# Attention blocks in chunk-major order with all keys on chip, and token sums through VectorE's bank ring

## The chip, the core and the metric
The kernel runs on one core of a Trainium2 chip. The metric is device time in microseconds of one execution. Three executions of the kernel before took 906.76, 907.65 and 915.72 us (median 907.65). The profiled execution took 914.75 us; its span, from the first to the last recorded instruction, is 913.0 us.

## The reference, cut to what matters
One transformer layer over 2048 tokens of width 256, all in float32. The input is normalised; on the normalised rows `xn` stand a causal attention with 16 heads of width 16 (rotary positions, softmax, output projection) and a mixture of experts (32 experts of inner width 128; six per token out of four of eight groups) with a shared expert:

```python
x = L0_attn_x                                  # (1, 2048, 256)
xn = _layernorm(x, axis=-1)
x = x + _L0_attn_ref(xn, Wqkv, Wout) + _L0_ffn_ref(xn, gate_w, w11, w33, w22, sw1, sw2, sw3)
# attention: softmax(causal(q k^T / 4)) v, heads merged, times Wout^T
# experts: sigmoid gates, six experts per token, silu(x w11) * (x w33) * c, times w22, summed
```

## The kernel before, in words
**Stages.** First the projections, tile by tile (16 tiles of 128 tokens), from 12 to 140 us of the profile. Queries and keys are rotated and each is split into three bf16 terms; these go to DRAM (`term_rows`) and come back transposed, as 96 rows of terms per head (`load_terms`, L420). Values stay in `v_all`. Then attention, in two lots with the experts between them: `attend(early)`, the experts, `attend(late)`.

**Attention.** Heads are worked in 4 groups of 4 (`g`), queries in 4 chunks of 512 (`c`), keys in blocks of 128 (`kb`). A key block of (g, c) has four score matmuls `st` (L1173, a mask by L1176 on the diagonal), each followed by an exponential on ScalarE (L710), and a value product `pv` (L1190, eight matmuls; weights are 32 columns of `V4`, the values of the group in hand). There are 160 blocks, here group by group: chunk (g, c) has 4(c+1) blocks. Before the blocks of a chunk its row maxima must be known. They come from `strips(g, c)`: score matmuls with queries as rows (`mx`, L1149, mask L1152) whose maxima VectorE takes (L955), 8(c+1) strips a chunk, 320 in all. `mc` combines them, `mt` turns them into three extra rows of the queries (copy L977). After the last block of a chunk ScalarE copies the sums (`oe`), TensorE turns them (`ot`), VectorE divides (L994, L996). At a change of group ScalarE copies the next group's values to `V4` (`take_v`, `v4`), and TensorE's first product of the group waits for it.

**The order.** All engines walk one list, written by `whole_order` (L96): between every two `st` steps stand those strips, token steps and output steps that are due by goals (`score_goals`, `token_goals`, `end_goals`), and two steps of a chain of routing and slot computation (`route`, `counts`, `ranks`, `slots`, `owner`; VectorE and TensorE in turn) until that is used up. The strips of chunk (0, 0) and eight chain steps stand ahead of the first block. Blocks are counted from 0 in this list. The experts stand before block 64.

**Banks.** Eight PSUM banks: two pairs as VectorE's ring (`d_ring`), banks 4 and 5 for `st` and the exponentials, bank 6 for value products, bank 7 for counts, ranks and, through blocks 8 to 50, the token sums. `banks_in_turn` (L186) gives bank 7 to the exponentials after the step `tokens`.

**Tokens.** GpSimd makes one-hot tiles from the slots (L568, L569, twelve instructions a token tile, four tiles of buffer). TensorE sums products of them over the 16 token tiles in bank 7 (`tok`, L1218, six matmuls a tile), VectorE casts the sum to `tok_i` (L1001). GpSimd's gathers of rows for the experts (L587) start from it. After the experts GpSimd adds the expert rows to `res` (L602). `oM` (L989) waits for them; these output steps begin at block 146.

**Buffers.** `turned` holds one group's queries and two groups' keys. SyncE loads the next group's queries chunk by chunk when `used` (L432) says the old ones are done, and the keys a group ahead.

## Time and profile before

| | us |
|---|---|
| median of three executions | 907.65 |
| profiled execution, its span | 914.75, 913.0 |
| projections until the first exponential | 0 to 144.2 |
| blocks 0 to 63 | 144.2 to 394.6 |
| experts | 394.6 to 617.7 |
| blocks 64 to 159 and the end | 617.7 to 913.0 |
| busy TensorE, VectorE, GpSimd, ScalarE | 836.4, 605.6, 505.1, 497.1 |

Busy time is recorded time of instructions; TensorE's matmuls are pipelined, so its rows overlap and include some waiting. The number after `x` is a count. A time in square brackets or after the bar is the idle time of the engine before the instruction, with what ended it. `PEclk` is TensorE's granted clock as a share of 2.4 GHz.

### The profile page before, as it was taken

The numbers are of one execution on the slowest core, as the hardware profiler recorded it, in microseconds if no ns is written. First come the engines' busy times: TensorE is split into PE (matmuls) and PEld (weight loads), VectorE is DVE, ScalarE is ACT, GpSimd is POOL, SyncE is SP. The second block draws the span as 40 slices with busy tenths as digits, with TensorE's granted clock in tenths as the row PEclk, the third lists the DMA queues.
The fourth block names the chain that finished last, engine by engine and source line by source line (L and its number), as shares of the span: only waits on it lengthen the run. The fifth ranks groups of instructions, "written<-read, shape, count | busy, mean of one in ns | idle before, by whom it ended". The sixth has DMA issues, their size and how long they took to land.

```text
span 913.0 us, 17558 instructions
## 1 busy us (share of the span) xinstructions
PE 836.4 (92%) x5281; PEld 455.5 (50%) x5282; DVE 605.6 (66%) x1179; ACT 497.1 (54%) x1214; POOL 505.1 (55%) x651
## 2 busy tenths in 40 slices
PE   5799977698989998989999999998999999999997
PEld 2466644233343433368888887773343343433444
DVE  2677776888876686755555555555788777888322
ACT  3556523155556655635444544456676756667672
POOL 3566640499989302046666666626878888810000
PEclk9999987799999999999999999999999999999999
DMA  7025554610000212037777777774585555510011
GB/s 222 1 78 175 172 175 138 165 32 19 1 19 1 67 44 64 1 102 229 234 234 227 225 244 229 140 140 71 74 170 87 72 90 72 88 18 1 13 35 47
DMA packets 81986, 96.15 MB, mean 105 GB/s; under 512 B 13030, under 2 KB 73446, under 8 KB 81894
## 3 DMA queue, kind: packets, MB, share of 16 engines
q0 software_dynamic: 19968, 31.47, 19.1%
q1 hardware_dynamic: 45033, 46.80, 17.3%
q10 hardware_dynamic: 16896, 16.78, 5.4%
q8 instruction: 45, 0.74, 0.3%
q14 instruction: 44, 0.36, 0.1%
HBM read 61.11 MB, written 33.82 MB: 104 GB/s over the span
## 4 chain that ended last, share of the span: by engine, by line
PE 68%; issue 14%; DVE 10%; SPq 2%; ACT 2%; DVEq 1%; DMA 1%; POOLq 1%; POOL 1%; ACTq 0%
PE bank L1190 13%; PE bank L1173 13%; PE vector_banks L1149 11%; PE vector_banks L1268 7%; DVE mpart L955 7%; PE vector_banks L1041 5%; PE vector_banks L1062 4%; PE bank L1281 3%; PE bank L1062 3%; PE bank L1041 2%; PE vector_banks L1210 2%; PE bank L1078 2%; PE bank L1176 1%; PE vector_banks L1152 1%; ACT probs L710 1%
## 5 line engine op out<-in xcount | busy, mean ns | idle before, releaser
L955 DVE TENSOR_REDUCE mpart<-vector_banks 128x2 f32<-128x1024 f32 (+3 forms) x320 | 330.7, 1062 | 100.8 <-PE vector_banks L1149 58.2
L710 ACT ACTIVATE probs<-bank 128x512 f32<-128x512 f32 (+3 forms) x428 | 213.5, 537 | 136.7 <-PE bank L1176 64.7
L1173 PE MATMUL bank<-turned 99*128 99x512 bf16 (+3 forms) x640 | 207.2, 355 | 17.4 <-ACT probs L710 5.3
L587 POOL DMA_INDIRECT turned<-normed_rows,tok_i x128 | 125.6, 981 | 138.6 <-PE vector_banks L1041 85.1
L1149 PE MATMUL vector_banks<-turned 96*128 96x512 bf16 (+3 forms) x640 | 185.3, 360 | 12.8 <-DVE mpart L955 12.2
L602 POOL DMA_INDIRECT res<-expert_rows,slot_i x96 | 148.9, 1551 | 43.3 <-issue 28.6
L1173 PEld LDWEIGHTS bank<-turned 99*128 99x128 bf16 x640 | 58.9, 97 | 186.2 <-ACT probs L710 86.6
L710 ACT ACTIVATE at_first<-bank 128x512 f32<-128x512 f32 (+3 forms) x212 | 106.2, 532 | 74.4 <-PE bank L1176 35.6
L1268 PE MATMUL vector_banks<-xn_all,probs 128*128 x512 | 136.3, 389 | 3.0 <-issue 1.3
L1190 PE MATMUL bank<-probs,V 128*32 128x512 f32 (+3 forms) x856 | 102.2, 549 | 0.0
L1268 PEld LDWEIGHTS vector_banks<-xn_all,probs 128*128 128x128 f32 x512 | 87.8, 191 | 16.0 <-issue 7.7
L1019 DVE SCALAR_TENSOR_TENSOR probs<-probs,vector_banks 128x128 f32<-128x128 f32 x128 | 36.9, 288 | 83.9 <-ACT probs L724 46.6
L615 ACT ACTIVATE probs<-bank 128x128 f32<-128x128 f32 (+1 forms) x256 | 83.5, 328 | 16.2 <-PE bank L1281 1.9
L724 ACT ACTIVATE probs<-vector_banks 128x128 f32<-128x128 f32 x128 | 35.6, 278 | 102.4 <-PE vector_banks L1268 85.4
L1149 PEld LDWEIGHTS vector_banks<-turned 96*128 96x128 bf16 x640 | 59.3, 101 | 59.0 <-DVE mpart L955 24.8
L568 POOL TENSOR_SCALAR turned<-turned 128x128 f16<-128x128 f16 x96 | 58.0, 604 | 45.4 <-DVE turned L936 42.2
L569 POOL TENSOR_SCALAR turned<-turned 128x128 f16<-128x128 f16 x96 | 76.9, 801 | 0.0
L1281 PE MATMUL bank<-xn_all,probs 128*128 x256 | 76.7, 382 | 0.0
L1013 DVE COPY probs<-vector_banks 128x256 f32<-128x256 f32 x128 | 53.5, 418 | 1.9 <-PE vector_banks L1041 1.3
L1176 PE MATMUL bank<-mask_k,identb 128*128 128x128 bf16 x256 | 54.6, 223 | 0.0
L1152 PE MATMUL vector_banks<-mask_q,identb 128*128 128x128 bf16 x256 | 53.5, 228 | 0.0
L1023 DVE SCALAR_TENSOR_TENSOR probs<-probs,slot_w,vector_banks 128x128 f32<-128x128 f32 x128 | 44.6, 348 | 10.8
(152 smaller groups left out, 967.8 us busy)
## 6 DMA issues: line engine op xcount, KB each, us to landing
expert_rows<-probs ACTq DMA_DIRECT2D x32, 512.0 KB
term_rows<-at_first SPq DMA_DIRECT2D x96, 128.0 KB
turned<-term_rows SPq DMA_DIRECT2D x32, 384.0 KB, 5.0
xn_all<-wexp SPq DMA_DIRECT2D x32, 384.0 KB
normed_rows<-xn_all SPq DMA_DIRECT2D x4, 512.0 KB, 5.5
turned<-normed_rows,tok_i POOLq DMA_INDIRECT x128
out<-res SPq DMA_DIRECT2D x16, 128.0 KB, 1.7
res<-x SPq DMA_DIRECT2D x1, 1536.0 KB, 9.2
```

The costliest lines, as they stand in the source:

```text
L569: last = gp.tensor_scalar(hi_hot[t % HOT][:, j, :], count_from_0[:, :], hi[:, t, j:j + 1], token[:, t:t + 1], ALU.is_equal, ALU.mult)
L587: gp.indirect_dma_start(xg[:, n % XR, :], None, xn_dram, bass.IndirectOffsetOnAxis(ap=tok_i[:, n:n + 1], axis=0)).then_inc(rows_in[n % XR] ...
L602: gp.indirect_dma_start(res[:, t, :], None, yg_dram, bass.IndirectOffsetOnAxis(ap=slot_i[:, t, j:j + 1], axis=0), compute_op=ALU.add).then ...
L615: return A(dst, src, ACT.Copy)
L710: A(PT[v // 2 % 6][:, v % 2, 0:width], bank[A_BANK[step][0]][:, 0:width], ACT.Exp).then_inc(s["scalar_bank_read"], 1)
L955: V.tensor_reduce(mpart[:, t % TPC, 2 * j:2 * j + 2, p], ring[:, :, 0:w], AX.X, ALU.max).then_inc(s["vector_bank_read"], 1)
L1041: return nc.tensor.transpose(dst, src, eye)
L1149: last = mm(ring[:, h, 0:w], q_turned(slice(0, KQ), 2 * j + h, t * P, P), k_turned(par, slice(0, KQ), 2 * j + h, p * CH, w), start=True, s ...
L1173: last = mm(ring[:, 0:CH - off], k_turned(parity(g), slice(0, KM), h, kb * P, P), q_turned(slice(0, KM), h, c * CH + off, CH - off), start ...
L1190: last = mm(pv_bank[VW * h:VW * (h + 1), off:CH], V4[:, kb, h, :], PT[(2 * v + h // 2) % 6][:, h % 2, 0:CH - off], start=kb == 0, stop=kb ...
L1268: last = mm(bank[2 + n % 2][:, 0:2 * INTER], xgT[n % 2][:, c, :], wt_flat[:, bass.ds(at + c * D, D)], start=c == 0, stop=c == DC - 1)
L1281: mm(bank[6 + n % 2][:, 0:D], ehT[n % 2][:, :], wt_flat[:, bass.ds(at + 2 * D, D)], start=True, stop=True).then_inc(s["y_done"], 1)
```

## The change
Key blocks go chunk by chunk: for each chunk c all four groups, then the next chunk. The keys of all groups and chunks have room of their own (`keys`); queries lie in four slots (`queries`, slot = (4c + g) mod 4), and a slot is loaded again when the blocks of the chunk four back are issued. The values are written once, by the projections, in rows of 17 words a head (16 values and a one), so `V4`, its copies and `v4` go; a value product takes 32 columns from a head's start. Token sums go through VectorE's ring: eight steps, each two token tiles in a ring bank, added to `tok_sum` by VectorE. Bank 7 goes to the exponentials after the last slot step, which stands at block 2. Goals are new: token steps from block 8 to 64; strips by chunk; experts before block 72. SyncE's loads are in the order of the new use. Buffers of early stages lie in other places. `V` of VectorE's program is called `VE`. The core of the diff:

```diff
-TOKENS_FROM, TOKENS_TO = 8, 50
-EXPERTS_AT = (1, NCH - 1)
+TOKENS_FROM, TOKENS_TO = 8, 64
+EXPERTS_AT = (2, NCH - 2)
...
-    key_blocks = [(g, c, kb) for g in range(NG) for c in range(NCH) for kb in range(TPC * (c + 1))]
+    key_blocks = [(g, c, kb) for c in range(NCH) for g in range(NG) for kb in range(TPC * (c + 1))]
     scores, score_goals = [], [(0, 0)]
...
+    for c in range(NCH):
+        for g in range(NG):
+            if c or g:
+                scores += strips(g, c)
+                if c == 0 or g in (0, NG - 1):
+                    score_goals.append((4 * key_blocks.index((g, c, 0)) - 6, len(scores)))
+    tokens = [("tok", u) for u in range(NT // 2)]
...
-            if pending[1] == NCH - 1:
-                order.append(("v4", pending[0] + 1))
...
-        if step[0] == "tokens":
+        if step == ("slots", SLOT_PIECES - 1):
             free.insert(0, 7)
...
-                copy(v_all[:, bass.ds(t, 1), :].rearrange("p a n -> p (a n)"), bank[3 + b][:, 0:D])
+                copy(V[:, t, 0:H * V1].rearrange("p (h v) -> p h v", v=V1)[:, :, 0:DH],
+                     bank[3 + b][:, 0:D].rearrange("p (h d) -> p h d", d=DH))
...
-                            last = mm(pv_bank[VW * h:VW * (h + 1), off:CH], V4[:, kb, h, :],
+                            last = mm(pv_bank[VW * h:VW * (h + 1), off:CH], V[:, kb, (HG * g + h) * V1:(HG * g + h) * V1 + VW],
...
+                    elif step[0] == "tok":
+                        u = step[1]
+                        dve.wait_ge(s["vector_bank_full"], n + 1)
+                        dve.drain()
+                        if u == 0:
+                            VE.tensor_copy(tok_sum[:, :], ring[:, 0, 0:SLOT_TILES]).then_inc(s["vector_bank_read"], 1)
+                        else:
+                            VE.tensor_tensor(tok_sum[:, :], tok_sum[:, :], ring[:, 0, 0:SLOT_TILES], ALU.add).then_inc(s["vector_bank_read"], 1)
+                        if u == NT // 2 - 1:
+                            dve.drain()
+                            VE.tensor_copy(tok_i[:, :], tok_sum[:, :]).then_inc(s["tok_ready"], 1)
...
+                if quarter == 0:
+                    sp.wait_ge(s["terms_stored"], 16 * STORES)
+                    for g in range(NG):
+                        load_keys(g, 0)
+                        load_queries(g, 0)
...
+            sp.wait_ge(s["terms_stored"], 16 * STORES * 4)
+            sp.wait_ge(ones_in[0], 16)
+            for c in (1, 2):
+                for g in range(NG):
+                    load_keys(g, c)
+                set_ones(c)
+                if c == 1:
+                    store_weights(3)
...
+            def next_queries(some):
+                for i in some:
+                    used(*chunks[i - Q_SLOTS])
+                    load_queries(*chunks[i])
+
             sp.wait_ge(s["plan_ready"], 1)
+            sp.wait_ge(s["weights_stored"], 16 * 4)
+            next_queries([Q_SLOTS])
+            for g in range(NG):
+                load_keys(g, NCH - 1)
+            set_ones(NCH - 1)
...
-                        if t == 0:
-                            pe.wait_ge(s["owner_row_ready"], 1)
-                        pe.wait_ge(s["hot_made"], t + 1)
-                        for j in range(TOPK):
-                            last = mm(gu_bank[:, 0:SLOT_TILES], lo_hot[t % HOT][:, j, :], hi_hot[t % HOT][:, j, :],
-                                      start=t == 0 and j == 0, stop=t == NT - 1 and j == TOPK - 1)
-                        last.then_inc(s["hot_used"], 1)
+                        u = step[1]
+                        for t in (2 * u, 2 * u + 1):
+                            pe.wait_ge(s["hot_made"], t + 1)
+                            for j in range(TOPK):
+                                last = mm(ring[:, 0, 0:SLOT_TILES], lo_hot[t % HOT][:, j, :], hi_hot[t % HOT][:, j, :],
+                                          start=t == 2 * u and j == 0, stop=t == 2 * u + 1 and j == TOPK - 1)
+                        last.then_inc(full, 1)
```

## Rows read from the trace of the kernel before

**Rows 1.** The page: busy time by engine, clock in 40 slices, one DMA group.
```profile
PE 836.4 (92%) x5281; PEld 455.5 (50%) x5282; DVE 605.6 (66%) x1179; ACT 497.1 (54%) x1214; POOL 505.1 (55%) x651
...
PEclk9999987799999999999999999999999999999999
...
turned<-term_rows SPq DMA_DIRECT2D x32, 384.0 KB, 5.0
```

**Rows 2.** Busy time by stretch: from:to, length, engines (count), clock, DMA share, GB/s.
```profile
144.20:179.70 35.50, 24.54 (x153) 11.44 (x153) 26.72 (x62) 7.00 (x16) 8.32 (x13) 0.76 0.62 176
...
258.00:339.90 81.90, 76.52 (x579) 31.13 (x578) 59.70 (x75) 50.82 (x101) 44.52 (x67) 1.00 0.14 33
...
737.40:810.10 72.70, 69.30 (x522) 28.40 (x521) 58.32 (x73) 49.15 (x102) 53.99 (x35) 1.00 0.52 77
810.10:900.00 89.90, 87.89 (x603) 37.20 (x601) 44.41 (x62) 61.83 (x131) 0.00 (x0) 1.00 0.06 19
```

**Rows 3.** The exponentials (L710) alone by stretch: ScalarE's busy time and count.
```profile
144.20:195.80 51.60, 16.12 (x33) 0.80 0.49 143
...
258.00:339.90 81.90, 48.50 (x97) 1.00 0.14 33
...
737.40:810.10 72.70, 47.09 (x98) 1.00 0.52 77
```

**Rows 4.** The strips' maxima (L955) alone by stretch: VectorE's busy time and count.
```profile
144.20:195.80 51.60, 30.66 (x31) 0.80 0.49 143
195.80:227.70 31.90, 23.33 (x23) 1.00 0.05 14
...
258.00:339.90 81.90, 50.85 (x50) 1.00 0.14 33
...
737.40:810.10 72.70, 50.14 (x49) 1.00 0.52 77
```

**Rows 5.** The timeline of the opening: start, duration, instruction, idle before it.
```profile
152.15 3.40 PE L1232 MATMUL bank<-at_first,onesb 128*128 128x480 bf16 x15 [1.78 <-DVE at_first L893]
...
160.35 3.00 SPq L423 DMA_DIRECT2D turned<-term_rows  x6
...
171.38 0.62 POOL L568 TENSOR_SCALAR turned<-turned 128x128 f16<-128x128 f16 x1 [42.15 <-DVE turned L936]
```

**Rows 6.** Groups of instructions, 144.2 to 195.8: count, busy us, mean ns, idle before.
```profile
L1149 PE MATMUL vector_banks<-turned 96*128 96x512 bf16 (+3 forms) x64 | 20.8, 403 | 5.9 <-DVE mpart L955 5.9
...
L955 DVE TENSOR_REDUCE mpart<-vector_banks 128x2 f32<-128x1024 f32 x20 | 24.0, 1222 | 9.7 <-PE vector_banks L1149 9.3
L955 DVE TENSOR_REDUCE mpart<-vector_banks 128x2 f32<-128x768 f32 x3 | 2.9, 950 | 0.1
L955 DVE TENSOR_REDUCE mpart<-vector_banks 128x2 f32<-128x512 f32 x4 | 2.8, 688 | 0.7 <-PE vector_banks L1152 0.6
L955 DVE TENSOR_REDUCE mpart<-vector_banks 128x2 f32<-128x256 f32 x4 | 1.7, 420 | 0.5 <-PE vector_banks L1152 0.4
```

**Rows 7.** The timeline at the first change of group.
```profile
317.08 1.05 ACT L615 ACTIVATE V<-v_all 128x1024 f32<-128x1024 f32 x1
...
318.57 0.28 PE L1173 MATMUL bank<-turned 99*128 99x256 bf16 x1 [1.05 <-ACT at_first L710]
```

**Rows 8.** Groups of GpSimd, 170 to 340, and TensorE's token matmuls, 258.0 to 339.9.
```profile
L569 POOL TENSOR_SCALAR turned<-turned 128x128 f16<-128x128 f16 x96 | 76.9, 801 | 0.0
L568 POOL TENSOR_SCALAR turned<-turned 128x128 f16<-128x128 f16 x96 | 58.0, 604 | 45.4 <-DVE turned L936 42.2 <-PE bank L1218 3.2
...
L1218 PE MATMUL bank<-turned 128*128 128x128 f16 x54 | 4.5, 218 | 0.0
```

**Rows 9.** Value weight loads of a block (timeline), and VectorE's division group, 640 to 800.
```profile
200.74 0.16 PEld L1190 LDWEIGHTS bank<-probs,V 128*32 128x32 f32 x8 [0.42 <-ACT probs L710]
...
L996 DVE TENSOR_TENSOR v_all<-vector_banks,rden 128x256 f32<-128x256 f32 x5 | 2.1, 425 | 0.4
```

**Rows 10.** VectorE's timeline after the token list is made.
```profile
347.85 0.42 DVE L955 TENSOR_REDUCE mpart<-vector_banks 128x2 f32<-128x256 f32 x1 [2.83 <-issue]
```

More of the change, by code:

```diff
@@ L160, in whole_order @@
                 values(block)
-            order.append(later.pop()[1])
+            order += [step for _, step in later]
+            later.clear()
             pending = []
@@ L257, in carve @@
             return take
-        turned = sb("turned", [P, 2 * HG * T])
+        KW = NG * HG * CH // 2
+        keys = sb("keys", [P, NCH * KW])
+        queries = sb("queries", [P, Q_SLOTS * HG * CH // 2])
         probs = sb("probs", [P, 4 * 2 * CH])
-        QW = HG * T // 2
-        EARLY_WORDS = 15360
-        first_words = sb("at_first", [P, EARLY_WORDS])
-        at_first = carve(first_words, EARLY_WORDS)
-        before = carve(turned[:, 2 * QW:3 * QW], QW)
-        routing = at_first
-        counting = carve(turned[:, 3 * QW:], QW)
-        ffn = carve(turned[:, 3 * QW:], QW)
+        o_words = sb("o_words", [P, NT * D])
+        more_words = sb("more_words", [P, 3840])
+        spare = sb("spare", [P, 3456])
+        at_first = carve(o_words, NT * D)
+        staging = [carve(keys[:, c * KW:(c + 1) * KW], KW) for c in (2, 1)]
+        routing = carve(keys[:, 3 * KW:], KW)
+        before = carve(more_words, 3840)
+        counting = carve(spare, 3456)
+        ffn = carve(spare, 3456)
         before_probs = carve(probs, 4 * 2 * CH)
@@ L276, in layer @@
         qk = [at_first([P, 2 * D]) for b in range(2)]
-        split = [at_first([P, SPLIT, 2 * D], BF16) for b in range(2)]
+        split = [staging[b]([P, SPLIT, 2 * D], BF16) for b in range(2)]
         left = at_first([P, 2 * D])
-        staged = [at_first([P, SPLIT, COLS, CH], BF16) for b in range(2)]
-        v_all = sb("v_all", [P, NT, D])
-        o_all = v_all
+        staged = [staging[b]([P, SPLIT, COLS, CH], BF16) for b in range(2)]
+        V = sb("values", [P, NT, VROW])
+        o_all = o_words[:, :].rearrange("p (t d) -> p t d", d=D)
         ident = sb("ident", [P, P])
@@ L447, in _ @@
                                          staged[quarter % 2][:, n, 2 * kind + half, :]).then_inc(s["terms_stored"], 16)
-                sp.wait_ge(s["terms_stored"], 16 * STORES * (quarter + 1))
-                for kind in range(2):
-                    load_terms(kind, 0, quarter)
+                if quarter == 0:
[3 more added lines that the diff above has]
+                        load_queries(g, 0)
             def load(e, b, first=False):
@@ L475, in _ @@
                 load(b, b, True)
-            for c in range(NCH):
-                used(0, c)
-                load_terms(0, 1, c)
-            for c in range(NCH):
-                load_terms(1, 2, c)
-            for c in range(NCH - 1):
-                used(1, c)
-                load_terms(0, 2, c)
+            ready = chunks.index(EXPERTS_AT) + Q_SLOTS
+            next_queries(range(Q_SLOTS + 1, ready))
             with sp.Fori(1, E // NB) as i:
@@ L486, in _ @@
                     load(NB * i + b, b)
-            used(1, NCH - 1)
-            load_terms(0, 2, NCH - 1)
-            for c in range(NCH):
-                load_terms(1, 3, c)
-            for c in range(NCH):
-                used(2, c)
-                load_terms(0, 3, c)
+            next_queries(range(ready, len(chunks)))
             for t in range(NT):
@@ L791, in shared_add @@
                 row = res[:, bass.ds(t, 1), :].rearrange("p a n -> p (a n)")
-                V.tensor_tensor(row, row, bank[6][:, 0:D], ALU.add).then_inc(s["shared_added"], 1)
+                VE.tensor_tensor(row, row, bank[6][:, 0:D], ALU.add).then_inc(s["shared_added"], 1)
             def statistics(tiles, part):
@@ L832, in route @@
                 for t in each:
[L833 removed]
+                    VE.max(out=top[:, t, :], in_=gx[:, t, :])
                 dve.drain()
```

242 lines of the change are left out of this document (113 added, 129 removed).

## The prediction, made before the changed kernel was run
> **What bounds the kernel now.** I read the page first. TensorE is busy 92% of the span, more than any other engine, and its clock is granted in full except at slices 9 to 12 [rows 1]. So the span is TensorE's own instruction stream plus the places where that stream stands still, and the question is where it does. I cut the attention into stretches by counting exponentials, four for each key block (a count of 97 or 98 is 24 blocks and one or two caught at the edges). Blocks 0 to 7 take 51.6 us, blocks 8 to 15 take 31.9, blocks 24 to 47 take 81.9 (27.3 for each eight) [rows 3, 4]. The same 24-block pattern (the last chunk of one group, then the first two of the next) returns after the experts, in blocks 104 to 127, and takes 72.7 us there. There the exponentials own three banks; before block 50 they own two. In both stretches VectorE reduces 49 or 50 strips for about 50.5 us [rows 4], and TensorE's busy share is 0.93 and 0.95 [rows 2]. So TensorE is paced by bank returns as much as by its work.
>
> The opening is another thing. Of its first 35.5 us TensorE has work for 24.5, at a mean clock of 0.76 [rows 2]. VectorE carries 31 strips in blocks 0 to 7, 20 of them of the widest form at 1222 ns, besides the chain of routing and slot steps; TensorE stands 5.9 us before strips for want of a returned bank [rows 4, 6]. The chain crosses between the two engines, the 15 rank matmuls take 3.40 us, and GpSimd gets its slots only at 171.38 [rows 5].
>
> **The change, term by term.** Total strips, exponentials and value products are the same; only their order changes, so each term is a stall removed or added. Terms are given with a value and both ends.
>
> Opening, blocks 0 to 7: **-14 us (-5 to -16)**. Counted from the new order, 19 strips stand beside these blocks instead of 31: eight of group 1, eight of group 2, three of group 3, all of chunk 0. By the forms' means (1222, 950, 688 and 420 ns, [rows 6]) they cost VectorE 14.7 us where it now spends 30.7 [rows 4]: 16 us less. The low end is the 5.9 us that TensorE visibly stands before strips, less one for what stays. I take nearly the high end, since VectorE works 26.7 of the first 35.5 us and the chain runs through it [rows 2]; 2 us stay with the waits for ranks and counts.
>
> Giving back the strips: **+8 us (+4 to +13)**. By block 16 the old order has done 54 strips beside blocks, the new one 43. Eleven wide strips must be done later. The price of a strip in a full stretch: blocks 8 to 15 have 23 strips and take 31.9 us, a third of the stretch of blocks 24 to 47 has 16.7 and takes 27.3, so 4.6 us for 6.3 strips, 0.73 us each, 8 in all. Ends: 0.4 us if only TensorE's columns count, 1.22 if VectorE's whole duration does.
>
> Third bank for blocks 8 to 49: **-10 us (0 to -16)**. The pair of stretches differs by 9.2 us in 24 blocks. The early one also holds 54 token matmuls (nine tiles; I take 0.056 us from start to start of these 128-column ones, so 3.0 us) [rows 8] and a strip more (0.5). These 5.7 us are 0.24 us for a block, 10 for 42 blocks. The high end is all 9.2 us (0.38 a block), the low end is nothing, if VectorE's ring is what binds.
>
> Group copies of values: **-3 us (0 to -3.2)**. Three times, at a change of group, ScalarE copies the group's values for 1.05 us in line with exponentials, and TensorE stands 1.05 us before its next score matmul [rows 7]. They go. The strided copy into the new layout in the projections takes the old copy's place on ScalarE; I cost it at nothing.
>
> Token sums in VectorE's ring: **+3 us (0 to +5)**. There are eight sums. The nearest row is a VectorE pass over 256 columns at 425 ns [rows 9]; with its drain say 0.5, 4 us of VectorE, most of which TensorE feels, since each also takes a ring place ahead of a strip. Behind the waiting sum on VectorE stand strips and maxima, and for these TensorE waits in turn. The 96 token matmuls stay.
>
> Uneven strips: **+2 us (0 to +5)**. The new goals put four strips to a block in blocks 11 to 14, three in 39 to 46, 2.7 in 83 to 94: 24 above the even two. The old order has the same 24 surplus, in blocks 0 to 23. Only the spacing is new, hence little.
>
> First token sum: **+2 us (0 to +5)**. It now needs two tiles of one-hots before block 8 goes on. GpSimd needs 12 instructions of 604 and 801 ns a tile, 8.4 us, 16.9 for two, after the slots are ready [rows 8]. Blocks 3 to 7 are small ones that take some 15 us by this sum. TensorE would stand the rest, with strips and exponentials queued behind.
>
> At nothing: SyncE's loads. It issues six loads of keys in 3.00 us [rows 5]; the new order has eight after the first quarter, hidden by the wait for the next quarter's terms, and later eight keys ahead of chunk 1's strips, which begin at block 10, some 20 us on. Chunk 3's keys, four weight loads and the queries follow, each for a use tens of us away; without that cover a load would cost its 5.0 us from issue to landing [rows 1]. The experts start at block 72 instead of 64: that moves the combining of rows on GpSimd some us later, but GpSimd is idle from 810.1 on [rows 2], so outputs that begin at block 146 still find them done. The stall when the gathers start after the token list (VectorE stands 2.83 us before 347.85) merely moves [rows 10].
>
> The sum is -14 + 8 - 10 - 3 + 3 + 2 + 2 = **-12 us**. The profiled execution took 914.75 us (span 913.0), 7.1 above the median of 907.65; a like execution would take 902.75, and the median becomes **895.7 us**.
>
> **A rule on the clock.** TensorE's granted clock is 0.76 over the first 35.5 us of the opening, a mean of its levels of 1.2 and 2.4 GHz, in a stretch where it is busy 69% [rows 2]; elsewhere it is 1.00. The Trainium skill (TensorE: Matmul & The Clock Gate, What's actually happening) says that the throttled state is the default and activity releases it. By that rule, taking strips out of the opening makes TensorE idler there, and the remaining work would run at 1.2 GHz for longer. An estimate by it: some 18 us of TensorE work left beside blocks 0 to 3 at 0.76 would be 27 at 0.50, and with half of the 9 us showing, 4 of the first term are lost, a sum of -8. I keep -12 because VectorE is what TensorE waits for there.
>
> **Rivals.** (a) *VectorE sets the pace, the third bank gives nothing.* For it: VectorE is busy 59.7 of 81.9 us in the two-bank stretch [rows 2], and idle TensorE time before strips names it. Against: the fast stretch has the same strips. Then the third term is 0: -2, **905.7 us**. (b) *More than forecast*: the whole 9.2 us is the banks' (-16) and strips come back at 0.4 us (+4): -22, **886 us**. For it: TensorE's busy records cover waits. Against: the token matmuls are real work. (c) *Slower, by the value rows.* The value products' weights come from rows 68 bytes apart by head instead of from an aligned block. Eight loads now take 0.16 us a block [rows 9]. If these doubled on TensorE's path, 160 blocks add 26 us: -12 + 26 = +14, **921.7 us**. Slower by over 1% needs 21 us, 0.13 a block. Against: they overlap the products. The Trainium skill (SBUF — State Buffer, Door 1: The DMA port swizzle) puts a penalty on each new 16-byte line; an estimate by it is nine lines for eight, 3 us in all. No row here shows that. (d) *Not what it says.* The third bank needs the slot chain's end, which is at block 2 in the order; if a wait held it back the time is that of (a).
>
> **Chances.** Forecast 0.50 (own range 888 to 903), (a) with (d) 0.27, (b) 0.12, (c) 0.11. About 1% (9 us) is what a measurement here can tell from no change. Faster by more: below 898.6, about 0.7 of the forecast, all of (b), a little of (a): 0.50. Slower by more: (c) and the bad ends of the terms: 0.12. Same: 0.38. The range with 8 in 10 runs from (b)'s 886 to **909**, leaving out (c) and the tail below (b).
>
> **What would show it.** Blocks 0 to 7 at 38 us (wrong above 47); 24 blocks with two strips a block before the experts at 75 us instead of 82, with token sums in them; no copies of values and no stand after them; GpSimd's first one-hot near 162 (some 9 of the opening's 14 us lie ahead of it). Wrong: eight value weight loads above 0.25 us; TensorE waiting for keys or queries; one wait of over 5 us at the first token sum; late stretches slower than 24.5 us for eight blocks.

## The result and the profile after

The changed kernel takes **911.42 us** (median of 20 executions, 908.07 to 917.19) against 908.03 for the kernel before (20 executions). The ratio is 1.0036 (95%: 1.0020 to 1.0051). The forecast was 895.7. So nothing was gained, and by the ratio some 3 us were lost, less than counts as a change here. The profiled execution took 912.08 us, its span is 910.2.

The two spans, 913.0 and 910.2, seem to tell of a gain. They don't: the profiled execution of before, 914.75 us, lies 6.7 above its kernel's median. A second one took 907.21 us (span 905.3). The largest difference between the two is in blocks 48 to 55. By stretch (from:to, length, then busy time and count of TensorE, its weight loads, VectorE, ScalarE and GpSimd, clock, DMA share, GB/s), first the execution that the prediction read:

```profile
339.90:367.70 27.80, 23.91 (x158) 8.74 (x156) 17.41 (x19) 14.98 (x35) 8.95 (x13) 0.94 0.21 58
```

and the same eight blocks in the second execution:

```profile
338.50:360.10 21.60, 21.60 (x161) 8.42 (x159) 17.12 (x19) 14.89 (x33) 8.96 (x13) 1.00 0.27 75
```

These 6.2 us belong to one execution and not to the kernel.

**Where the time went.** The start of the first exponential of a block, by counting exponentials as in [rows 3], gives this ledger (us; in brackets the second profiled execution of each kernel, where it differs by more than 1):

| blocks | before | after | difference |
|---|---|---|---|
| 0 to 7 | 51.6 (51.2) | 35.8 (39.5) | -15.8 (-11.7) |
| 8 to 15 | 31.9 | 34.6 | +2.7 |
| 16 to 31 | 58.2 (60.0) | 50.9 (52.6) | -7.3 |
| 32 to 47 | 54.0 | 62.5 (60.4) | **+8.5** (+6.5) |
| 80 to 95 | 45.6 | 56.9 | **+11.3** |
| 96 to 127 | 96.5 | 94.4 | -2.1 |

The rest is -3.3 (+1.6) for blocks 48 to 79 with the experts and +3.5 (+2.1) from block 128 to the end. At block 32 the changed kernel is 20 us ahead (17 in the second pair). It loses most of them in two stretches of 16 blocks.

Equal block numbers are not equal work everywhere. A diagonal block has narrower matmuls and exponentials than a full one. Of blocks 0 to 31, 8 are full in the new order and 20 in the old (0 and 4 of blocks 0 to 7); the new order has four more full ones in each of blocks 48 to 79, 96 to 127 and 128 to 159. So a part of the 20 us is work put off, and no run here prices it alone. In blocks 32 to 47 and 80 to 95 both orders have 8 full and 8 diagonal blocks, so those two rows compare like with like. The page after, to be laid beside [rows 1]:

```profile
PE 832.5 (91%) x5281; PEld 460.8 (51%) x5282; DVE 604.1 (66%) x1187; ACT 494.1 (54%) x1210; POOL 502.6 (55%) x651
...
PEclk9999988999998999989999999998999999999998
...
keys<-term_rows SPq DMA_DIRECT2D x16, 384.0 KB, 8.8
```

All engines work about as long as before. What is new is in the clock's row. The 7, 7 at slices 7 and 8 of before are gone (an 8, 8 stands at slices 6 and 7), but there is an 8 at slices 13, 18, 28 and 40, where there was none: at 273 to 296 us, in the dense blocks 32 to 47, on both sides of the experts, and at the end. By stretch, the kernel after:

```profile
143.90:179.70 35.80, 27.60 (x260) 15.99 (x259) 25.25 (x70) 13.66 (x34) 17.77 (x27) 0.90 0.79 206
179.70:214.30 34.60, 29.44 (x272) 15.22 (x269) 29.10 (x43) 14.56 (x35) 34.13 (x51) 1.00 0.36 96
214.30:265.20 50.90, 47.16 (x385) 21.31 (x384) 37.42 (x51) 30.82 (x67) 39.84 (x60) 1.00 0.06 17
...
327.70:376.90 49.20, 46.63 (x345) 18.96 (x343) 37.44 (x46) 33.32 (x67) 8.95 (x13) 1.00 0.15 41
...
652.50:709.40 56.90, 52.05 (x363) 20.41 (x361) 48.28 (x55) 30.66 (x66) 47.75 (x31) 0.97 0.55 80
```

In the second profiled execution of the changed kernel, blocks 0 to 7 and 32 to 47 read:

```profile
142.00:181.50 39.50, 30.64 (x261) 17.66 (x259) 25.38 (x70) 13.74 (x34) 18.46 (x28) 0.80 0.82 205
268.30:328.70 60.40, 51.84 (x401) 22.37 (x399) 47.66 (x59) 32.31 (x68) 37.39 (x55) 1.00 0.05 14
```

So the opening's clock of 0.90 (first row of the stretches) belongs to one execution, and blocks 32 to 47 are long (60.4 us) at full clock too. Blocks 80 to 95 before:

```profile
668.00:713.60 45.60, 44.31 (x337) 18.46 (x335) 38.73 (x45) 32.07 (x69) 36.25 (x24) 1.00 0.70 128
```

The strips' maxima alone, after (VectorE's busy time and count), to be read against [rows 4]:

```profile
143.90:179.70 35.80, 14.34 (x19) 0.90 0.79 206
...
214.30:265.20 50.90, 31.03 (x33) 1.00 0.06 17
265.20:327.70 62.50, 41.12 (x41) 0.95 0.04 14
652.50:709.40 56.90, 43.31 (x41) 0.97 0.55 80
```

and the two stretches of before that the last two replace:

```profile
285.90:339.90 54.00, 36.02 (x34) 1.00 0.19 45
668.00:713.60 45.60, 34.83 (x33) 1.00 0.70 128
```

The stretches that lost time are those that got more strips: 41 in 16 blocks instead of 34 and 33. VectorE is busy 48.3 of 56.9 us there. Blocks 96 to 127, with two strips a block in both kernels, take 2.1 us less than before.

**What stands in such a stretch.** The longest stand of the exponentials in the trace after is at the end of chunk (2, 1): diagonal blocks, whose score matmuls are the smallest, with the widest strips between them, and the turning of the next chunk's maxima right behind. The timelines of TensorE, VectorE and ScalarE (start, duration, instruction, idle before it):

```profile
288.05 0.23 PE L1175 MATMUL vector_banks<-keys,queries 96*128 96x128 bf16 x1 [1.61 <-DVE mpart L975]
...
289.18 1.87 PE L1068 MATMUL vector_banks<-identb,mcat 128*3 128x128 bf16 x16 [0.72 <-DVE mpart L975]
...
286.78 2.67 DVE L975 TENSOR_REDUCE mpart<-vector_banks 128x2 f32<-128x1024 f32 x3
...
291.41 0.28 ACT L734 ACTIVATE probs<-bank 128x128 f32<-128x128 f32 x1 [4.66 <-PE bank L1199]
```

TensorE's instructions stand in the trace in the order of the list. A strip that waits for a ring bank holds back the next score matmul behind it, and ScalarE, with three banks free, stands 4.66 us. A third exponential bank can't help here: what holds the score matmul up is ahead of it in the queue. The bank comes late because VectorE has just combined the next chunk's maxima (L984 to L993, 285.39 to 286.86) and then has three of the widest maxima, 2.67 us, to take. In this execution TensorE, having stood 1.61 and 0.72 us, goes on at a lower clock:

```profile
288.00:291.00 3.00, 2.23 (x21) 1.84 (x22) 1.45 (x2) 0.00 (x0) 3.00 (x6) 0.59 0.00 0
291.00:296.00 5.00, 5.00 (x29) 1.74 (x32) 3.20 (x3) 1.31 (x4) 3.24 (x5) 0.56 0.11 30
```

Clock 0.56 is close to 1.2 of 2.4 GHz: by an estimate from this row (5.00 times 0.56), what TensorE does in these last 5 us would take some 2.8 at full clock. The second execution has the same stands, 1.60 and 0.72 us, and no slow stretch behind them; its turn of the maxima takes 1.05 us instead of 1.87, and ScalarE stands 3.73 us:

```profile
292.24 1.05 PE L1068 MATMUL vector_banks<-identb,mcat 128*3 128x128 bf16 x16 [0.72 <-DVE mpart L975]
```

The stand belongs to the order, the dip to the execution. The dip is worth about 2 of the 8.5 us; 6.5 remain without it.

### The profile page after: what moved, and what is told of

The parts are those of the page before. It is cut to its first block, busy times and chain, and to the rows that moved or that the text cites. A ratio compares the mean times of both kernels' runs of the same rounds, so it can differ in the third digit from the quotient of the medians.

```text
span 910.2 us, 17585 instructions
## 1 busy us (share of the span) xinstructions
PE 832.5 (91%) x5281; PEld 460.8 (51%) x5282; DVE 604.1 (66%) x1187; ACT 494.1 (54%) x1210; POOL 502.6 (55%) x651
## 4 chain that ended last, share of the span: by engine, by line
PE 75%; DVE 14%; issue 4%; DMA 3%; DVEq 2%; POOLq 1%; ACT 1%; POOL 0%; SPq 0%; ACTq 0%
PE bank L1212 14%; PE bank L1196 12%; PE vector_banks L1289 12%; DVE mpart L975 10%; PE vector_banks L1175 10%; PE vector_banks L1068 7%; PE bank L1302 6%; PE vector_banks L1089 4%; PE bank L1089 3%; PE bank L1068 2%; DMA xn_all<-wexp 2%; PE vector_banks L1232 2%; DVEq L983 2%; PE bank L1105 2%; PE vector_banks L1178 1%
## 5 line engine op out<-in xcount | busy, mean ns | idle before, releaser
L975 DVE TENSOR_REDUCE mpart<-vector_banks 128x2 f32<-128x1024 f32 (+3 forms) x320 | 326.6, 1061 | 93.3 <-PE vector_banks L1175 72.5
L734 ACT ACTIVATE probs<-bank 128x512 f32<-128x512 f32 (+3 forms) x428 | 215.8, 541 | 125.5 <-PE bank L1199 73.9
L1196 PE MATMUL bank<-queries,keys 99*128 99x512 bf16 (+3 forms) x640 | 205.5, 354 | 8.4 <-DVE owner_row L960 3.5
L614 POOL DMA_INDIRECT spare<-normed_rows,tok_i x128 | 125.3, 979 | 130.3 <-PE vector_banks L1068 84.1
L1175 PE MATMUL vector_banks<-keys,queries 96*128 96x512 bf16 (+3 forms) x640 | 182.7, 355 | 13.5 <-DVE mpart L975 10.4
L734 ACT ACTIVATE more_words<-bank 128x512 f32<-128x512 f32 (+3 forms) x212 | 106.4, 526 | 86.0 <-PE bank L1199 60.1
L1196 PEld LDWEIGHTS bank<-queries,keys 99*128 99x128 bf16 x640 | 61.2, 97 | 172.0 <-ACT probs L734 75.7
L1212 PE MATMUL bank<-probs,values 128*32 128x512 f32 (+3 forms) x856 | 104.7, 561 | 0.0
L595 POOL TENSOR_SCALAR spare<-spare 128x128 f16<-128x128 f16 x96 | 57.3, 597 | 65.4 <-DVE spare L956 33.0
L1175 PEld LDWEIGHTS vector_banks<-keys,queries 96*128 96x128 bf16 x640 | 60.1, 100 | 62.5 <-DVE mpart L975 22.7
L596 POOL TENSOR_SCALAR spare<-spare 128x128 f16<-128x128 f16 x96 | 76.2, 794 | 0.0
```

The lines of the kernel that those rows point to most:

```text
L596: last = gp.tensor_scalar(hi_hot[t % HOT][:, j, :], count_from_0[:, :], hi[:, t, j:j + 1], token[:, t:t + 1], ALU.is_equal, ALU.mult)
L614: gp.indirect_dma_start(xg[:, n % XR, :], None, xn_dram, bass.IndirectOffsetOnAxis(ap=tok_i[:, n:n + 1], axis=0)).then_inc(rows_in[n % XR] ...
L734: A(PT[v // 2 % 6][:, v % 2, 0:width], bank[A_BANK[step][0]][:, 0:width], ACT.Exp).then_inc(s["scalar_bank_read"], 1)
L975: VE.tensor_reduce(mpart[:, t % TPC, 2 * j:2 * j + 2, p], ring[:, :, 0:w], AX.X, ALU.max).then_inc(s["vector_bank_read"], 1)
L1175: last = mm(ring[:, h, 0:w], q_turned(slice(0, KQ), g, 2 * j + h, t * P, P), k_turned(slice(0, KQ), g, 2 * j + h, p * CH, w), start=True, ...
L1196: last = mm(ring[:, 0:CH - off], k_turned(slice(0, KM), g, h, kb * P, P), q_turned(slice(0, KM), g, h, c * CH + off, CH - off), start=True ...
```

## The experiments

The theories. **Spacing**: the strips bunched in blocks 32 to 47 and 80 to 95 eat the gain, since VectorE takes over 1 us for each and blocks with fewer strips give nothing back. **Bank**: the third bank is worth less than forecast. **Lateness**: strips end only a few score steps ahead of their chunk, and the turn of maxima waits. Ratios are to the kernel before in the same round on the same chip, with the 95% interval; 0.001 is 0.9 us.

**The changed kernel again**, as the measure for the first four.

> The changed kernel itself, unchanged, so that the others have a time and a trace of it on the same chip. Both theories: 1.003 to 1.005 of the kernel before, within 3 us of it.

Measured: 913.11 us, 1.0046 (1.0024 to 1.0068).

**Even strips.** Most goals are left out, so that the planner spreads the strips evenly between those that stay: 17 or 18 for each eight blocks from block 16 to 95, nowhere more than 10 for four, where the changed kernel has up to 12. It also has four strips more in blocks 0 to 7 (23) and three fewer in blocks 8 to 15 (21).

```diff
-                if c == 0 or g in (0, NG - 1):
+                if (g, c) in ((1, 0), (0, 1), (0, 2), (0, 3), (NG - 1, NCH - 1)):
```

> The changed kernel with the strips spread evenly: goals only at chunks (1,0), (0,1), (0,2), (0,3) and (3,3), so that from block 16 no eight blocks hold more than 18 strips (the changed kernel has 22 in blocks 40 to 47, and 20 and 20 in 80 to 95). Theory A (above some 2.3 wide strips a block VectorE sets the pace, and each surplus strip costs its whole 1.22 us or more, which sparse stretches do not give back): 8 to 16 us faster than the changed kernel, about 897; blocks 32 to 47 take 54 us instead of 62.5, blocks 80 to 95 take 48 to 50 instead of 56.9. Theory B (the loss is TensorE's work moved out of the opening and costs the same wherever it stands): within 3 us of the changed kernel, about 911.

Measured: 902.57 us, 0.9926 (0.9902 to 0.9949), so 0.0120 or **10.9 us** below the changed kernel on the same chip, and faster than the kernel before. It was run twice more on another chip:

> The evenly spread kernel once more, unchanged, as the base of the other three on this chip, and for a trace nearer its median (the first was of its slowest execution). Expected: 0.990 to 0.996 of the kernel before, blocks 32 to 47 at 54 us, 80 to 95 at 50 us.

> The evenly spread kernel, unchanged, on the chip of the three below: their base. 0.988 to 0.994 of the kernel before.

Measured: 898.30 us, 0.9875 (0.9844 to 0.9905), and 901.55 us, 0.9921 (0.9892 to 0.9950). Each of its three profiled executions was the slowest of its series (910.66, 903.21 and 905.57 us), so its traces rather understate the gain. By stretch, blocks 0 to 7, 8 to 15, 16 to 31, 32 to 47, 48 to 63 of the second:

```profile
145.60:184.40 38.80, 29.65 (x275) 17.23 (x273) 28.14 (x74) 13.72 (x33) 20.78 (x31) 0.91 0.81 204
184.40:216.60 32.20, 27.39 (x256) 14.02 (x254) 27.06 (x40) 14.30 (x35) 31.75 (x48) 1.00 0.30 85
...
216.60:269.10 52.50, 48.41 (x396) 22.01 (x397) 41.07 (x55) 30.32 (x66) 38.15 (x57) 1.00 0.06 16
269.10:323.70 54.60, 50.65 (x387) 21.64 (x386) 44.06 (x55) 30.78 (x66) 40.24 (x59) 0.97 0.06 16
323.70:373.40 49.70, 47.76 (x350) 18.88 (x349) 39.63 (x48) 32.72 (x66) 8.95 (x13) 1.00 0.16 40
```

and its maxima in blocks 32 to 47 and 80 to 95:

```profile
269.10:323.70 54.60, 37.84 (x37) 0.97 0.06 16
650.30:700.50 50.20, 37.29 (x35) 1.00 0.56 80
```

The gain is where it should be: 54.6 us instead of 62.5 (60.4 in the second execution) with 4 strips fewer, 50.2 instead of 56.9 with 6 fewer. What was moved into blocks 16 to 31 (37 instead of 33 strips, 2.3 a block) costs 52.5 - 50.9 = 1.6 us there, 0.4 a strip. The even kernel also turns some maxima earlier, 7 to 14 score steps ahead of their chunk where the changed one has 3; the last experiment takes that away.

**Bunching doubled.** The strips of chunks (2, 3) and (3, 3) are done in the first half of the blocks that precede them. The strips are the same in all, 61 or 62 in blocks 112 to 143.

```diff
-                if c == 0 or g in (0, NG - 1):
+                if (g, c) in ((2, NCH - 1), (3, NCH - 1)):
+                    score_goals.append((4 * key_blocks.index((g - 1, c, 0)) + 26, len(scores)))
+                    score_goals.append((4 * key_blocks.index((g, c, 0)) - 6, len(scores)))
+                elif c == 0 or g in (0, NG - 1) or (g, c) == (1, NCH - 1):
```

> The changed kernel with the strips of chunks (2,3) and (3,3) done in the first half of the blocks before them: blocks 109 to 119 and 125 to 134 get up to four strips a block, blocks 121 to 125 and 136 to 143 none; the work is the same. Theory A: some 19 strips above the pace, each 1.2 us of which the empty blocks give back 0.4 to 0.5: 12 to 20 us slower than the changed kernel. Theory B: within 3 us of it.

Measured: 936.54 us, 1.0306 (1.0279 to 1.0332), **23.6 us** above the changed kernel. Its blocks 112 to 119, 120 to 127, 128 to 135 and 136 to 143:

```profile
756.90:796.30 39.40, 32.02 (x184) 10.33 (x184) 32.32 (x36) 19.03 (x34) 33.00 (x22) 0.96 0.52 72
796.30:817.50 21.20, 18.82 (x126) 5.67 (x125) 4.57 (x5) 14.51 (x33) 9.37 (x7) 1.00 0.33 44
817.50:855.10 37.60, 30.51 (x187) 10.15 (x191) 32.03 (x36) 19.10 (x34) 0.00 (x0) 1.00 0.00 1
855.10:872.90 17.80, 16.22 (x112) 4.50 (x112) 0.00 (x0) 13.97 (x34) 0.00 (x0) 1.00 0.00 1
```

the maxima in the first:

```profile
756.90:796.30 39.40, 29.16 (x28) 0.96 0.52 72
```

(28 again in blocks 128 to 135, none behind them) and the same 32 blocks in the changed kernel:

```profile
756.90:849.70 92.80, 89.50 (x607) 33.00 (x606) 71.56 (x78) 65.34 (x131) 42.65 (x28) 1.00 0.29 42
```

116.0 us against 92.8, and this accounts for the whole loss. By the same eight blocks, the changed kernel takes 22.5, 24.7, 22.5 and 23.4 us, with 17, 17, 17 and 14 maxima taken in them. Eleven more cost 16.9 and 15.1 us, **1.4 to 1.5 each**: VectorE's 1.22 for the widest form [rows 6], and something more. Twelve and 14 fewer give back 3.5 and 5.6 us, 0.3 to 0.4 each, near the 0.4 at which the prediction put TensorE's columns. The price has a knee: up to about 2.3 strips a block (the even kernel above) a strip costs 0.4 us or less, at 3.5 a block more than its time on VectorE. Blocks 32 to 47 and 80 to 95 of the changed kernel, with up to three, stand on the dear side.

**The third bank withheld** until the last token step, in the changed kernel (a) and in the even one (b):

```diff
-        if step == ("slots", SLOT_PIECES - 1):
+        if step == ("tok", NT // 2 - 1):
```

> The changed kernel with bank 7 given to the exponentials only after the last token sum (block 57), not after the slots (block 2): the third bank taken away alone. If the third bank is worth what the prediction says (0.24 us a block): 10 to 13 us slower than the changed kernel, blocks 16 to 31 at 56 us instead of 50.9. If VectorE's ring sets the pace before the experts: within 2 us of the changed kernel.

> The even kernel with the third bank withheld until the last token sum (block 57). If the third bank's worth was hidden in the changed kernel by VectorE's dense stretches, it shows here: 5 us or more slower than the even kernel. If a third bank is worth little before the experts however the strips lie: 2 to 3 us slower, as in the changed kernel.

Measured: (a) 915.66 us, 1.0073 (1.0046 to 1.0101), beside the changed kernel's 1.0046: 2.5 us, with some 3 us either way by the two intervals. (b) 908.22 us, 1.0000 (0.9972 to 1.0028), beside the even kernel's 0.9875 in the same series: 11.3 us; beside its 0.9926 and 0.9921 in the two other series it would be 7. By stretch, (a), blocks 16 to 31, 32 to 47, 48 to 63:

```profile
215.50:268.10 52.60, 48.73 (x385) 20.40 (x383) 37.77 (x51) 31.78 (x66) 39.86 (x59) 1.00 0.06 16
268.10:330.90 62.80, 54.39 (x401) 22.46 (x399) 47.91 (x59) 32.87 (x67) 38.92 (x58) 0.97 0.05 13
330.90:383.80 52.90, 49.87 (x345) 19.04 (x343) 37.59 (x45) 34.22 (x66) 8.95 (x13) 0.97 0.14 39
```

(b), the same blocks:

```profile
219.00:274.60 55.60, 50.88 (x397) 21.63 (x397) 41.59 (x56) 31.79 (x66) 38.56 (x57) 1.00 0.05 15
274.60:331.40 56.80, 52.44 (x387) 21.74 (x386) 44.11 (x55) 32.02 (x66) 39.67 (x59) 0.97 0.05 15
331.40:383.20 51.80, 49.52 (x351) 18.64 (x349) 40.04 (x48) 33.63 (x67) 8.94 (x13) 1.00 0.15 39
```

By stretch the bank gives 1.7, 0.3 and 3.7 us in (a), in all 5.7, and 3.1, 2.2 and 2.1 in (b), in all 7.4. Against the second trace of the changed kernel (a) reads 0.1, 2.4 and 3.7. Without the bank TensorE stands 2.1 us before score matmuls in (a) and 4.2 in (b), between 180 us and the experts; with it 0.0 in both kernels. So the bank is worth less than forecast in the changed kernel, and more in the even one by the ratios. That dense strips are the reason fits this, but the stretches don't single them out, and single traces set the two only 2 us apart: it is likely and not shown.

**The ring and the bank in the old order**: the kernel before, group by group, with the token sums in VectorE's ring and bank 7 given away after the last slot step.

```diff
-    tokens = [("tok", t) for t in range(NT)] + [("tokens",)]
+    tokens = [("tok", u) for u in range(NT // 2)]
...
-        if step[0] == "tokens":
+        if step == ("slots", SLOT_PIECES - 1):
```

> The kernel before, group by group as it is, with one part of the change alone: token sums in eight steps through VectorE's ring, and bank 7 to the exponentials after the slots (block 3). By the prediction's terms (third bank -10 us, sums +3): 7 us faster than the kernel before, 0.992. If the third bank is worth only the 2.6 us that its removal from the changed kernel cost, against the same sums: within 2 us of the kernel before. Blocks 24 to 47 (81.9 us before) show it: 76 by the first, 80 to 82 by the second.

> The kernel before, profiled once more, since its first profiled execution lay 7 us above its median. Expected: a span of 905 to 908 us; the stretch of blocks 48 to 63, which held the stand at 347 us, 4 to 6 us shorter than the 54.7 us of the first trace; the opening within 2 us of 51.6.

Measured: 904.96 us, 0.9966 (0.9941 to 0.9990), **-3.1 us**, where the terms of the prediction give -7 (-10 and +3). The gain stands where there are two strips a block (24 to 47), none where there are nearly three (8 to 15):

```profile
197.50:229.70 32.20, 27.95 (x213) 11.68 (x212) 26.91 (x33) 15.70 (x34) 31.72 (x48) 1.00 0.05 14
259.90:337.80 77.90, 73.35 (x574) 30.95 (x573) 60.59 (x79) 48.68 (x101) 56.72 (x84) 1.00 0.17 44
```

against 31.9 and 81.9 us [rows 2 to 4] (83.4 in the second execution). In the 24 blocks from which the prediction read 5.7 us for the bank, bank and sums together give 4.0 (5.5), so that reading was sound; it did not hold for the other blocks.

**The chunk-major order alone, evenly spaced**: bank 7 keeps the token sums and goes to the exponentials after the last of them, at block 60.

```diff
-    tokens = [("tok", u) for u in range(NT // 2)]
+    tokens = [("tok", t) for t in range(NT)] + [("tokens",)]
...
-        if step == ("slots", SLOT_PIECES - 1):
+        if step[0] == "tokens":
```

> The evenly spread kernel with the token sums back in bank 7 and so only two banks for the exponentials until block 64: both halves of that part of the change undone together. By the prediction's terms: 8 to 10 us slower than the even kernel with ring sums, about 912. If bank and sums pay for each other: within 3 us of it, about 903.

Measured: 903.87 us, 0.9970 (0.9948 to 0.9993): the order alone gives -2.7 us. Ring and bank together bring 4 to 9 us more, by the even kernel's 0.9926, 0.9921 and 0.9875 in other series. It also stands 0.0030 below (b), which differs from it in that the sums go through the ring, and in that the bank comes at block 57, not 60: 2.7 us for the eight sums, though the intervals overlap and the two ran in different series.

**Goals counted in TensorE's time** instead of steps (a diagonal step weighs 0.6).

```diff
+    for g, c, kb in key_blocks:
+        pace += [pace[-1] + (i + 1) * (6 if kb >= TPC * c else 10) for i in range(4)]
...
-            upto = len(steps) if everything else max(done, due(goals, at))
+            upto = len(steps) if everything else max(done, due(goals, pace[at] if steps is scores else at))
```

> The evenly spread kernel with goals in TensorE's time instead of steps: a step of a diagonal block counts 0.6 of a step of a full one, so that the four diagonal blocks at a chunk's end, where VectorE also has the maxima and the turned rows, hold 5 to 7 strips and the full ones 9 to 11 for every four. If VectorE's load in short stretches sets the pace: 3 to 7 us faster than the even kernel, about 898. If eight-block evenness is all that counts: within 2 us of it, about 903.

Measured: 905.38 us, 0.9978 (0.9955 to 1.0001). That is worse than all three results of the plain even kernel. So leaving diagonal blocks fewer strips gains nothing.

**Strips back into the opening.** Even kernel with six strips moved from blocks 8 to 15 into blocks 0 to 7 (29 and 16 instead of 23 and 22).

```diff
+    score_goals.insert(2, (22, 24))
```

> The even kernel with the 24 strips of chunk 0 due by block 5 instead of block 10: blocks 0 to 7 hold 29 strips, not 23, and blocks 8 to 15 hold 15, not 21; all else alike. If strips in the opening cost VectorE's time there (the prediction's first term) and blocks 8 to 15 are held by VectorE too, the two cancel: blocks 0 to 7 about 5 us longer, 8 to 15 about 5 us shorter, in all within 2 us of the even kernel. If the opening's gain is real gain and the later blocks don't give back: 3 to 5 us slower than the even kernel.

Measured: 903.17 us, 0.9943 (0.9924 to 0.9963), 6.2 us above the even kernel of that series, 2 above it by the two others. Its two stretches:

```profile
146.40:197.70 51.30, 38.19 (x312) 22.31 (x311) 35.88 (x86) 13.97 (x34) 32.38 (x48) 0.81 0.73 185
197.70:222.40 24.70, 22.93 (x223) 11.96 (x220) 19.50 (x28) 13.68 (x35) 19.48 (x30) 1.00 0.17 50
```

Beside 38.8 and 32.2 us: +12.5 and -7.5, so 2.1 us a strip in the opening (clock 0.81 against 0.91) and 1.25 in blocks that have nearly three each. But the even kernel's two other traces have 42.5 and 42.6 us for blocks 0 to 7, at clock 0.81, and 33 to 34 us for 8 to 15; beside these it is about +9 and -9, 1.5 us a strip on both sides. So a strip costs more than its time on VectorE in both places. The ratios make the emptier opening a gain of 2 to 6 us; the traces leave it between 0 and 5, according to the clock that the opening got.

**Goals two blocks earlier**, the dense stretches kept (as many strips in them as in the changed kernel), and **both cures together**.

```diff
-                    score_goals.append((4 * key_blocks.index((g, c, 0)) - 6, len(scores)))
+                    ahead = 6 if c == 0 or (g, c) == (0, 1) else 14
+                    score_goals.append((4 * key_blocks.index((g, c, 0)) - ahead, len(scores)))
```

> The changed kernel with its dense stretches kept, but every goal from chunk (1,1) on eight steps earlier, so that maxima are turned 6 to 11 score steps ahead of their first use, not 3. Rival to theory A: the even kernel gained because maxima are ready earlier. Then this is 5 us or more faster than the changed kernel, below 908. By theory A only density counts: within 3 us of the changed kernel (about 1.004 of the kernel before); blocks 32 to 47 and 80 to 95 stay at 59 to 62 and 56 us.

> The changed kernel with dense stretches kept and goals eight steps earlier, unchanged from its first run (0.9893), as a repeat on this chip: 0.987 to 0.993. If it were 1.00 or more, its first result would not stand for the kernel.

> Both at once: even spread, and from chunk (0,2) on goals eight steps earlier, so maxima stand ready 11 to 22 score steps ahead. If density and lateness are two costs that add: 3 to 8 us faster than the even kernel, about 0.983. If both cures remove the same stand of TensorE at a chunk's end: within 2 us of the better of the two.

Measured: early goals 897.77 us, 0.9893 (0.9864 to 0.9922), and 898.45 us, 0.9905 (0.9874 to 0.9937): as good as even strips. The spacing theory alone forecast about 1.004 for them, so it is not the whole. Both together 903.00 us, 0.9937 (0.9903 to 0.9971): not better. The dense stretches with early goals, blocks 32 to 47 and 80 to 95:

```profile
265.20:324.10 58.90, 51.79 (x399) 22.02 (x398) 47.52 (x59) 32.02 (x66) 40.25 (x60) 1.00 0.05 14
645.90:699.80 53.90, 50.26 (x362) 19.37 (x360) 47.18 (x55) 31.20 (x67) 45.05 (x30) 1.00 0.54 79
```

3.6 and 3.0 us shorter than in the changed kernel, whose list has the same 40 strips in each, and at full clock; beside the changed kernel's second trace, at full clock too, the first is 1.5 us shorter. That is 6.6 of the 14.8 us between the two spans. Another 4.1 lie behind block 128, where this list has 25 strips left and the changed one 29. TensorE's groups between 180 and 400 us (count, busy, mean ns, idle before them), with early goals:

```profile
L1176 PE MATMUL vector_banks<-keys,queries 96*128 96x512 bf16 (+3 forms) x294 | 81.6, 346 | 9.1 <-DVE mpart L976 7.3 <-DVE o_words L1016 1.5
...
L1069 PE MATMUL vector_banks<-identb,mcat 128*3 128x128 bf16 x128 | 8.4, 219 | 3.1 <-DVE mpart L976 3.1
```

and in the changed kernel, 180 to 404:

```profile
L1196 PE MATMUL bank<-queries,keys 99*128 99x512 bf16 (+3 forms) x255 | 80.9, 344 | 0.0
L1175 PE MATMUL vector_banks<-keys,queries 96*128 96x512 bf16 (+3 forms) x286 | 80.5, 350 | 8.2 <-DVE mpart L975 6.4 <-DVE o_words L1015 1.4 <-DVE tok_sum L1025 0.2
L1068 PE MATMUL vector_banks<-identb,mcat 128*3 128x128 bf16 x128 | 9.3, 230 | 7.8 <-DVE mpart L975 7.8
```

The wait for strips stays; it is the wait at the turn of the maxima that falls, from 7.8 to 3.1 us. TensorE's stands for maxima add up to 17.3 us in the changed kernel, with 3.1 before the token matmuls (L1239); before they were 5.9 in the two groups that the old order has (1.7 and 4.2). Against that, its stands before score matmuls are gone (0.0 above). In the kernel before they were 9.7 us in the same stretch, and in its second execution:

```profile
L1173 PE MATMUL bank<-turned 99*128 99x512 bf16 (+3 forms) x238 | 78.3, 355 | 5.9 <-DVE turned L977 1.6 <-ACT at_first L710 1.5 <-DVE tok_i L1001 0.6
```

So the third bank did what it was meant to do, and TensorE stands before strips and turns instead.

**Even strips with late turns**: the turn is held back until three score steps ahead of its chunk, in all chunks.

```diff
-                    later.append((at + 4, ("mt", *step[1:3])))
+                    later.append((max(at + 4, 4 * key_blocks.index((*step[1:3], 0)) - 3), ("mt", *step[1:3])))
```

> The even kernel with its strips as they are, but the turning of each chunk's maxima (mt) held back to three score steps before the chunk, as in the changed kernel: lateness alone. If density alone is the cost: within 3 us of the even kernel. If lateness is: 5 us or more slower than the even kernel, near 1.00.

Measured: 898.26 us, 0.9890 (0.9845 to 0.9935), no slower than the even kernel in the same series (0.9921). A late turn costs nothing where its strips are done up to 18 score steps ahead, as here. My reading is that a dense stretch that runs into a late turn is what costs; take away either and the other is cheap, and that is why the cures don't add. It is a reading of the runs above and the timeline at 286 us; no run shows the queue at the turn by itself. A rival is untested: with early goals the turn still follows the last strip by four score steps, but these are steps of wider diagonal blocks, no longer the narrowest ones, so VectorE has more time for them.

## Why the prediction was wrong

Term by term, in the prediction's own order:

- **Opening, -14: right in size, in part by luck.** -15.8 and -11.7 us in the two pairs of executions, at clock 0.90 and 0.80. The term counts strips alone; that blocks 0 to 7 are all diagonal in the new order, where the old has four full ones, is in the measured gain and in no term. 19 strips stand in blocks 0 to 7 and take VectorE 14.3 us (14.7 forecast). GpSimd's first one-hot stands at 161.93 us (162 forecast), 9.4 us earlier than in [rows 5]. The third bank did cost a stand of 3.54 us, forecast at none: the first score matmul in it waits for the end of the slot chain.

```profile
161.93 0.61 POOL L595 TENSOR_SCALAR spare<-spare 128x128 f16<-128x128 f16 x1 [32.97 <-DVE spare L956]
...
162.07 0.28 PE L1196 MATMUL bank<-queries,keys 99*128 99x256 bf16 x1 [3.54 <-DVE owner_row L960]
```

- **The clock's estimate (-8 instead of -12): not borne out.** The opening's clock did not fall with fewer strips. Before it was 0.80 [rows 3] and 0.78 in the two executions, after 0.90 and 0.80, over a shorter stretch. TensorE was busy 76 and 79% of blocks 0 to 7 before, 77% (27.6 of 35.8 us) and 78% (30.6 of 39.5) after. The estimate had taken strips out and left the waits; the waits went with them, and the busy share stayed. The Trainium skill (TensorE: Matmul & The Clock Gate, What's actually happening) says that activity releases the throttle. These traces neither contradict nor settle that, since nearly the same busy share goes with 0.90 and with 0.80.
- **Giving back, +8 at 0.73 us a strip: too cheap where strips are dense.** 1.25 to 1.5 us in blocks 8 to 15 (six strips moved), 1.4 to 1.5 in the bunches, 0.3 to 0.4 up to some 2.3 strips a block. I took one slope across a knee. The slope also came from unlike blocks: half of blocks 8 to 15 are diagonal, a third of blocks 24 to 47.
- **Third bank, -10: failed.** 2.5 us by the ratios in the changed kernel (5.7 in a pair of traces), 3.1 together with the ring sums in the old order. In the even kernel it is 7 to 11, near the forecast. The price was read from stretches with two strips a block [rows 2, 4] and used for 42 blocks, about a third of which have more in the changed order. The step that failed is the transfer: the bank removes the stands before score matmuls (0.0 us left), but the stands before strips and turns grow from 5.9 to 14.2 us. Rival (a), in which VectorE's ring is what binds, named that wait.
- **Uneven strips, +2: failed, and this is the largest miss.** 10.9 us by the even kernel (1.0046 against 0.9926 in one series). The prediction counted 24 surplus strips in both orders and took the spacing as free. But the old order's surplus stands in blocks 0 to 23, where VectorE's chain and the opening were already paid for as "opening"; I took that gain at VectorE's price (-14) and put the same strips back at about half of it.
- **Group copies, -3:** the copies and the stands of [rows 7] are gone from the trace; not tried alone. **Token sums, +3:** 2.7 us by two runs of different series whose intervals overlap; TensorE stands 3.2 us before them, 3.1 of it for a ring bank. **First token sum, +2:** nothing; none of that wait is GpSimd's. **SyncE's loads, 0: right.** A load of keys lands after 8.8 us instead of 5.0 [rows 1], and TensorE waits for none in the trace.
- **Rival (c), value rows 68 bytes apart: refuted.** Eight loads still take 0.16 us [rows 9]:

```profile
201.15 0.16 PEld L1212 LDWEIGHTS bank<-more_words,values 128*32 128x32 f32 x8 [0.21 <-ACT probs L734]
```

The two failed terms miss by 8.9 and 7.5 us, together 16.4; between -12 and the measured +3.3 (0.0036 of 908) lie 15.3. That the two come so close is partly luck: they are not separate, giving back cost more than its +8 as well, and one kernel's executions spread by 9 us.

**The better versions.** Even strips (0.9875 to 0.9926), early goals (0.9893, 0.9905) and even strips with late turns (0.9890) beat the kernel before by about 1% and the changed one by more. Each is an edit of one or two lines in the order.

**What stays open.** Where the rest of the gain of early goals comes from (8 of 14.8 us lie outside the dense stretches), and how much of it is clock: over all executions their median clock is 0.983, the even kernel's 0.978 to 0.981, the changed one's 0.972 to 0.975. And why the even kernel varies by 0.005 between series, as wide as what would rank the three.

## What to carry to other kernels

The price of an operation added beside a busy engine is no constant: find the density at which the second engine takes over (here above 2.3 strips a block, 0.3 to 0.4 us below and over 1.2 above), and price what is moved on the side where it lands. Where two orders are compared by position, check that the same positions hold the same work. Where a planner spaces work by due times, look at its densest stretch before the change is timed; goals that are left out can be worth more than the reordering. Buffers for one consumer give less than they seem to while another consumer of the same queue holds it up (here 2.5 us instead of 10).

## What was unexpected of the hardware

Granted clock and time go together from one execution of one program to the next. Of the 20 executions of the changed kernel, those with a mean clock of 0.976 or 0.977 took 908.1 to 911.4 us, those at 0.970 to 0.974 took 911.5 to 913.7, those at 0.964 or 0.968 took 913.3 to 917.2. Past the opening, every dip in the two traces of the changed kernel follows a place where TensorE stood for one or two microseconds. The reverse does not hold: of its stands of over 1.3 us, those that end at 262, 325, 363, 663, 754 and 801 us in the first trace have no dip behind them, and the one at 288 us has none in the second. So which stands turn into a dip differs between executions, and an order that keeps TensorE from standing may gain the slow stretch with the stand. That it does is an inference from these places; no run removes one stand alone.
